# The last four rounds of an edge stage: weighing and sums ahead of the next round's gathers

## What is computed

```
xh = (h @ W).reshape(n, heads, d)
a_s = (xh * att_src).sum(-1)
a_d = (xh * att_dst).sum(-1)
alpha = leaky_relu(a_s[src] + a_d[dst], 0.2)
amax = segment_max(alpha, dst)
e = exp(alpha - amax[dst])
z = segment_sum(e, dst)
out = segment_sum(xh[src] * (e / z[dst])[:, :, None], dst)
```

## Time and profile before

| | us |
|---|---|
| runs of the kernel before: median | 7531.67 |
| lowest, highest of three | 7530.8, 7540.61 |
| the profiled execution | 7531.31 |
| its span in the trace | 7529.6 |
| DVE busy | 5498.7 (73%) |
| PE busy | 5390.2 (72%) |
| POOL busy | 5176.0 (69%) |
| mean granted clock of PE, share of full | 0.779 |

### The profile page before, as it was taken

How to read it: one execution, slowest core, us unless ns; L and a number is a source line. 1 busy time by engine, 2 the same in 40 slices (tenths; PEclk the granted TensorE clock), 3 DMA queues, 4 the chain that set the end, 5 groups by cost and what they waited for, 6 DMA issues and landing times. The chain is left out here.

```text
span 7529.6 us, 113108 instructions
## 1 busy us (share of the span) xinstructions
PE 5390.2 (72%) x23828; PEld 3495.0 (46%) x23829; DVE 5498.7 (73%) x16160; ACT 2138.7 (28%) x5415; POOL 5176.0 (69%) x5471
## 2 busy tenths in 40 slices
PE   5677777766775677777766666587777876673399
PEld 3344444444443345444544444355555544342398
DVE  6677777777777677777777778677787777778643
ACT  2112121211113233333321113234343421113466
POOL 1777777777774777777777773777777777772444
PEclk8777787877778777777777777678888877776599
DMA  6445455544443444444444444444444444444444
GB/s 211 138 141 145 141 146 141 144 135 140 136 134 116 117 121 123 121 123 122 122 114 111 111 110 139 115 123 128 126 128 125 127 118 111 111 111 139 146 70 64
DMA packets 531615, 949.93 MB, mean 126 GB/s; under 512 B 117850, under 2 KB 366049, under 8 KB 531030
## 3 DMA queue, kind: packets, MB, share of 16 engines
q0 software_dynamic: 259808, 691.84, 34.5%
q1 hardware_dynamic: 254610, 235.89, 10.2%
q10 hardware_dynamic: 16612, 15.96, 0.6%
HBM read 796.92 MB, written 151.73 MB: 126 GB/s over the span
## 5 line engine op out<-in xcount | busy, mean ns | idle before, releaser
L1250 POOL DMA_INDIRECT edges_G<-rows,edges_index x4980 | 4749.4, 954 | 1554.4 <-issue 1481.0
L1450 PE MATMUL edges_ps_o<-edges_G,edges_OH 128*128 128x264 f32 x9960 | 3507.1, 490 | 307.1 <-DVE edges_G L1726 173.9
L1450 PEld LDWEIGHTS edges_ps_o<-edges_G,edges_OH 128*128 128x128 f32 x9960 | 2119.1, 234 | 1127.4 <-issue 634.9
L1744 DVE TENSOR_TENSOR acc<-acc,edges_ps_o 128x264 f32 x2490 | 1048.8, 421 | 821.7 <-PE edges_ps_o L1450 547.6
L1726 DVE TENSOR_TENSOR edges_G<-edges_G,edges_ps_c 128x1024 f32<-128x1024 f32 x1245 | 1500.3, 1205 | 1.8 <-ACT edges_G L1270 1.3
L1294 ACT ACTIVATE edges_OHT<-edges_ps_far 128x512 bf16<-128x512 f32 x1245 | 742.5, 596 | 1331.2 <-PE edges_ps_far L1410 1330.8
L1418 PE MATMUL edges_ps_s<-ident,edges_alpha 128*128 128x128 f32 x249 | 114.4, 459 | 1266.5 <-DVE edges_alpha L1620 1266.5
L1718 DVE TENSOR_TENSOR edges_OH<-edges_ps_c,relT 128x512 f32<-128x512 f32 x1245 | 848.6, 682 | 0.1
L1602 DVE COPY edges_node<-terms 128x12 bf16 x2490 | 476.1, 198 | 292.1 <-issue 73.8
L1418 PEld LDWEIGHTS edges_ps_s<-ident,edges_alpha 128*128 128x128 f32 x249 | 44.2, 177 | 1375.3 <-DVE edges_alpha L1620 1375.3
L1410 PE MATMUL edges_ps_far<-edges_rels,pole_rows 5*128 5x512 bf16 x1245 | 608.4, 489 | 41.3 <-DMA WT<-in_L_mix_b 19.8
(11 more groups left out here) (377 smaller groups left out, 6211.3 us busy)
## 6 DMA issues: line engine op xcount, KB each, us to landing
edges_G<-rows,edges_index POOLq DMA_INDIRECT x4980
xslot<-edges_blank SPq DMA_DIRECT2D x80, 650.0 KB
edges_masks<-lanes_of SPq DMA_DIRECT2D x123, 192.0 KB
rows<-node_ext SPq DMA_DIRECT2D x147, 130.0 KB, 2.2
experts_X<-xslot SPq DMA_DIRECT2D x105, 130.0 KB, 2.1
node_rows<-rows SPq DMA_DIRECT2D x98, 130.0 KB
h<-node_Hn SPq DMA_DIRECT2D x98, 128.0 KB, 1.7
W<-in_L_ffn_W SPq DMA_DIRECT2D x16, 512.0 KB
```

What stands on the lines that cost most here:

```text
L1250: g.indirect_dma_start(G[n][:, s, 0:RW], None, dr["rows"], bass.IndirectOffsetOnAxis(index[n][:, s:s + 1], 0)).then_inc(gathered[n], 16)
L1450: mm = pe.matmul(ps_o[BANK_OF[g]][:, 0:GW], OH[:, 2 * g + j, :], G[n][:, 2 * g + j, :], start=(j == 0), stop=(j == 1))
L1744: v.tensor_tensor(a, a, ps_o[BANK_OF[g]][:, 0:GW], ALU.add).then_inc(added, 1)
```

## The change

A constant STRAIGHT = 3 marks rounds 80, 81 and 82. DVE's special order, now called `straight_on`, is used in steps 79, 80 and 81 (whenever the next round is a marked one) and not only in step 81. In steps 80 and 81 it leaves out the adds of groups 8 and 9 of the round before and the last pack of one-hots, as the step before has done them. PE's branch goes the same way: it holds `spread_fade`, the ten sums with the five `distances` of round w+2 among them, `spread_ad` of round w+2 behind group 6, and at the end `turn` and `turn_back` of round w+1. `load_node` of round 82 is kept, at the end of step 79. ACT's `fades` no longer waits for the turn of the next round where that comes later (steps 79 and 80). PE's `turn` waits for the round's own predecessor's fade, and `spread_ad` of rounds 81 and 82 for one scan fewer. Nothing is added to or taken from what is computed.

```diff
+STRAIGHT = 3
+        def straight(i, n):
+            return RING * i + n >= NW - STRAIGHT
...
-                if exists(i, n, 2):
+                if exists(i, n, 1) and not straight(*later(i, n, 1)):
                     a.wait_ge(turned, w + 2)
...
-                wait_past(pe, ran, w)
+                wait_past(pe, ran, w - 1 if straight(i, n) and straight(*later(i, n, -1)) else w)
...
-                wait_past(pe, fade_ready, w if last_window(i, n) else w - 1)
+                wait_past(pe, fade_ready, w if straight(i, n) else w - 1)
...
-                if exists(i, n, 1) and last_window(*later(i, n, 1)):
-                    sums(*later(i, n, -1), range(8, 10))
+                if exists(i, n, 1) and straight(*later(i, n, 1)):
+                    if not straight(i, n):
+                        sums(*later(i, n, -1), range(8, 10))
                     spread_fade(i, n)
-                    sums(i, n, range(WG))
+                    for g in range(FAR):
+                        sums(i, n, [g])
+                        if exists(i, n, 2):
+                            distances(*later(i, n, 2), g)
+                    sums(i, n, range(5, 7))
+                    if exists(i, n, 2):
+                        spread_ad(*later(i, n, 2))
+                    sums(i, n, range(7, WG))
                     turn(*later(i, n, 1))
                     turn_back(*later(i, n, 1))
                     return
...
-                if one and last_window(*next1):
-                    before_last(i, n, prev, next1, blocks)
+                if one and straight(*next1):
+                    straight_on(i, n, prev, next1, blocks)
                     return
...
-                for g in (8, 9):
-                    add(*prev, g, next(block_ends[0]))
-                onehots(i, n, 4)
+                if not straight(i, n):
+                    for g in (8, 9):
+                        add(*prev, g, next(block_ends[0]))
+                    onehots(i, n, 4)
...
                 place_drops(*next1)
+                if exists(i, n, RING - 1):
+                    load_node(*later(i, n, RING - 1))
```

More of the change, by code:

```diff
@@ L1912, in step, with straight_on @@
                     load_node(*later(i, n, RING - 1))
-            def before_last(i, n, prev, next1, blocks):
+            def straight_on(i, n, prev, next1, blocks):
                 differences(i, n)
```

## The result

| | kernel before | changed kernel |
|---|---|---|
| median of 9 runs | 7530.88 | 7552.75 |
| lowest, highest | 7527.76, 7540.61 | 7538.38, 7556.31 |
| the profiled execution | 7531.31 | 7538.38 |
| its span | 7529.6 | 7536.6 |

The ratio is 1.0024, with a 95% interval of 1.0013 to 1.0034. The medians are 21.9 us apart, the ratio says 18. The change is slower. The interval reaches from 10 to 26 us, so it doesn't tell whether the loss passes the 15 us that the prediction called slower. The forecast was 7538 with a range up to 7551. By the ratio the changed kernel has 7549, inside the range, and its median of 7552.75 lies just above it. The profiled execution is the fastest of the nine and understates the loss.

A forecast was written before the change was run, and what follows sets the result against it. POOL's gather issue paces a stage, DVE and PE its tail. Steps and scans of 19.2 + 7.1 + 20.0 + 4.6 + 17.7 = 68.6 us against 66.6 add 6 us in three stages: 7538, range 7524 to 7551.

The forecast's parts named there:

- What bounds the tail: End of each edge stage: DVE, and PE where DVE waits for sums, is the bound; round 82's scores start 13.4 us late.
- The gather waits: DVE's waits for gathers of rounds 80 and 81 go to nothing, 4.7 us in the third stage.
- The sum: From step 79's start to round 82's scores: 68.6 us against 66.6, 2.0 us later a stage, 6 us in three.
- scans and copies behind it: Behind step 79: undivided scans of 4.6 us plus ten node copies, 2.5 us net of the turn back; 7.1 us.
- step 80: PE's clock surely falls in the gap ahead; from 16.1 us fast, 8.7 slow us make it 20.0 us.
- scans behind it: Undivided scans behind step 80: scores, turn, twelve dependent steps and turn back, 4.6 us.
- step 81: The clock falls in the 7.8 us gap ahead; 15.9 us plus a slow start give 17.7 us, bounds 15.9 and 19.
- the term for step 79: The clock falls ahead of step 79 in two stages of three: 20.0 or 17.65 us, on average 19.2.
- the remark that DVE can't hide a slow PE: In straight steps DVE's adds wait for PE's sums in order, so DVE can't hide PE's slow stretch.
- The price of 0.45 us for each slow us: In a straight step each us of PE at the slow clock adds 0.45 us, from 2.56 us against 1.41.
- The slow one: Steps 79 to 81 all begin slow for 12 us: 73.7 us, 7.1 us a stage later, 7553; chance 0.14.
- the rivals of a kind clock: Steps 79 to 81: short slow stretches, 7524.5, chance 0.24; or clock never falls, 7516, chance of gain over 0.2% 0.04.

The follow-up runs named there:

- s1: The changed kernel's source with STRAIGHT = 1, only step 81 in the new order, which is the order of the kernel before; ratio 1.0001 to the kernel before.
- warm: The changed kernel with idle matmuls on PE in the gaps from the end of step 78 to the end of step 81; ratio 0.9996 to the kernel before.
- the node experiment: The changed kernel with the ten node copies of round 82 moved from behind step 79's scans into its middle; ratio 1.0011 to the kernel before.

## Why the prediction was right or wrong

**What bounds the tail: right.** DVE and PE set it, the gathers did not move, and no mark was reached ahead of the last landing.

**The gather waits: right.** They are gone in steps 79 and 80 in both traces of the changed kernel, in all stages.

**The sum: right in its sign, too small by more than half.** From step 79's start to the mark, on average over the six stages of the two traces of each order, it is 71.3 us in the new order and 66.2 in the old one (before and s1). That is 5.1 us a stage, 15 in three, where the forecast had 2.0 and 6. The tails differ by 17.6, because step 79 also began 1.0 us a stage later against the last gather than in the old order, which the forecast didn't have and whose cause is open, and what follows the mark took 0.3 less. By terms, mean of the six stages:

| term | forecast | measured |
|---|---|---|
| step 79 | 19.2 | 20.7 (19.8 to 22.5) |
| scans and copies behind it | 7.1 | 7.9 (7.8 to 8.1) |
| step 80 | 20.0 | 20.2 (18.7 to 21.0) |
| scans behind it | 4.6 | 4.6 |
| step 81 | 17.7 | 18.0 |
| sum | 68.6 | 71.3 |

By what DVE did in that stretch, mean of the six stages of each order:

| | old order | new order |
|---|---|---|
| DVE busy | 49.9 | 51.8 |
| waits for gathers | 4.7 | 0 |
| waits for PE's sums | 7.9 | 14.9 |
| other idle time | 3.7 | 4.6 |
| sum | 66.2 | 71.3 |

So the saved wait came back as 7.0 us more waiting for PE, and 1.9 us more busy time. The 119 instructions of the stretch are the same, and their durations add up to some 57 us in either order, but they overlap less when a chain is not divided.

**The step that failed is the term for step 79, the clock in it and the length that it starts from.** I took the clock to fall in two stages of three, from one gap of 4.2 us against one fall after 3.7. It fell in all six stages. In five of them it fell in the gap, 3.0 to 4.0 us behind the end of the last sum of round 78, as it did ahead of the row at 6756.97. There the prediction had the cause right and only the share of stages too low. In the stage shown first it fell at about 6747.4, while PE was at the last sums of round 78, and before the gap had begun. There was no rest to explain it, only a spell of thin work. Had I put all stages slow, step 79 would have had 20.0, and it measured 20.7. The 20.0 starts from 16.1 us, the length without the adds of the round before, though step 79 has them. With a fast clock it takes 17.65 to 18.0 us (`warm`). The slow stretches behind the first sum were 6.2 to 12.1 us, 8.4 on average, near my 8.7. So they cost 2.8 us and not 3.9, and the remark that DVE can't hide a slow PE was wrong in this step.

**Step 80 was right by luck.** With a fast clock it takes 16.6 us and not 16.1, and the slow stretches behind its first sum were 7.7 us on average and not 8.7. The two errors nearly cancel: 20.2 measured, 20.0 forecast. The price of 0.45 us for each slow us holds there (3.5 us for 7.7).

**Slips in the rows.** The first stage of the kernel before takes 67.3 us, not 67.4. The rise that stands as 4478.3 is 4478.5 by its own average of 0.87, so the short slow stretch is 3.9 us and not 3.6; neither changes the forecast. The change does not make two more bursts that start slow: in the rows themselves steps 79 and 80 of the kernel before start with sums of 2.10 us, and only step 81 is new.

**The copies.** I subtracted the turn back that they hide from their 2.70 us. The trace shows 2.77 us and in front of them 0.59 us of issue that the kernel before doesn't have at that place. Probably the longer instructions ahead cover it in the old order, and the short scans don't. That the idle time went with the move in the node experiment agrees with this, but it was not tested by itself.

**Baseline.** The average of 66.6 us from one execution was fair: the other trace of the old order has 65.8.

**The rivals.** The slow one (steps at half clock, 73.7 us a stage, 7553) was nearest to the measured time, and its mechanism is what was found: PE at half clock takes the place of the gather wait. I gave it 0.14, since I counted as its condition the longest slow stretches in all steps, which did not come. The gain that the rivals of a kind clock forecast came only with idle matmuls.

The Trainium skill, page "VectorE: DVE Perf Modes", section "The DRAIN you can't avoid", says that the semaphore costs nothing extra. The traces neither bear out the 9 us that I drew from it nor contradict it for the scans. The undivided chain takes 4.57 us, 4.43 with a fast clock. Its instructions keep DVE busy for 3.7 us of that, 0.42 is the wait for PE's turn, and the idle time before a dependent one is 0.03 us each time. So by its own durations alone it would be some 0.4 us shorter and not 1.5. The idle time of 0.37 us stands between two adds into `acc`, which are not in the chain.

The warning of the Trainium skill (page "TensorE: Matmul & The Clock Gate", section "HAM oscillation — how this bites in real kernels") that bursts of matmuls behind long waits each start cold agrees with the traces. Filling one gap took 1.9 us off the step behind it.

## What to carry to other kernels

Before work is gathered ahead of a wait, look at what the wait hides on the other engines: here PE's bursts started at half clock in both orders, but the scattered scans and the wait for gathers gave PE time to catch up, and DVE's new order left only waits for PE's sums. Count the bursts of PE as a term of the sum, at the slow clock wherever the stretch ahead of one is thin and not only where it is empty, and put small copies where their engine waits anyway.

## What was not expected of the hardware

- The clock of PE fell while PE was still at work: in the 2 us from 6746 it was busy for 1.05 us, and no rest in the 2.5 us before the fall at 6747.4 was longer than 0.95 us. This is one of six stages; in the other five it fell in a gap.
- Idle matmuls on operands at hand pay for themselves: in the old order 9 us off the whole time by themselves, and with the node copies moved too 12 us in the new order, for 267 idle matmuls (1068 more instruction records, weight loads included: 114164 against 113096), without any change in what is computed.
- The node stage between the first and the second edge stage takes 131.4 to 135.3 us in the three traces of the old source and 136.6 to 140.5 in the nine of the new one, whatever their order of steps. The means are some 5 us apart, as much as the change in question costs in one edge stage. What sets it was left open.
